# A two-layer LoRA block on one core: the transposes of a factor product moved into one group

## The chip, the cores and the metric

The kernel runs on one core of a Trainium2 chip. The metric is the device time of one execution in microseconds (us). Engines are called TensorE (PE in the rows, PEld for its weight loads), VectorE (DVE), ScalarE (ACT), GpSimd (POOL) and SyncE (SP, whose queue issues most DMA transfers).

## The reference, cut to what matters

```python
def layer0(x, ids, W, b, As, Bs):            # x: (8, 256, 1024)
    A, Bm = As[ids], Bs[ids]                 # (8, 1024, 16), (8, 16, 1024)
    return x @ W.T + b + ((x @ A) @ Bm) * 2.0

def layer1(x, ids, W, b, A_w, B_w):          # x seen as (8, 256, 1024)
    A, Bw = A_w[ids], B_w[ids]               # (8, 16, 1024), (8, 1024, 16)
    return x @ W.T + b + (x @ A.T) @ Bw.T

x = x + layer0(x, ids0, W0, b0, A0, B0)
x = x + layer1(x, ids1, W1, b1, A1, B1)
```

This is the mathematics of it; the reference writes each layer out with einsums, all in fp32.

## The kernel before, in words

The kernel folds both layers into one. With U = I + W0 and V = I + W1 (transposed), the dense part of the result is x (U V), so the product of the two weights is made once, in a weight stage, and then each of the eight batches is multiplied with it. Both products follow the Strassen-Winograd scheme with seven products of 512 x 512 quadrants. fp32 accuracy comes from splitting every operand into a high part (a cast by ScalarE to the fp32r format) and a low part (a subtraction by VectorE), and three matmuls (high x high, high x low, low x high) for each tile. Functions named `high...` are ScalarE's casts, `low...` VectorE's subtractions, `combine` VectorE's sums of quadrants.

The order of work on each engine is written out by hand, one program per engine, tied by semaphores. There is no planner. TensorE's weight stage runs M1, M2, the first G passes (L1227), M7, four transposes, M3, the small product of the factors (L1252), the r passes for the low-rank rows (L1173 to L1175), three matmuls each onto those rows (L1268 to L1270), M6, the second G passes (L1282), M5, M4. Each M is four row blocks of twelve matmuls with 512 columns. Then come the column sums of the bias (L1427), the h products of batches 0 and 1 (L1337, x times the stacked low-rank factors), and the batches, whose products are in L1305 to L1307 and L1312.

**G** is the product of U and the second layer's A factors, gathered for all eight batches. It is made transposed: the G passes leave one half at a time in bank 4 (`b_banks[0]`). ScalarE copies the half to `gt_raw` (`gt_copy`, L501, L508), TensorE turns it 128 x 128 at a time with four transposes (`turn`, L1164, L1167), and VectorE copies the result from its bank into its half of `g_all` (`g_copy`, L761, L763). `gt_raw` is one place, the second half of `g_all`, used for both halves, so the second copy of ScalarE waits for the first four transposes. `turn(0)` stands after M7 (L1239) and writes bank 0, `turn(1)` in M4 after its second row block (L1296), into bank 7. The wait ahead of `turn(1)` is for one block of d22 and one of t1 (L1294, L1295), since M5's result leaves its banks in the order 3, 1, 2, 0 (`ORDER_LAST`): ScalarE makes d22's high part (L647), VectorE its low part (L799) and t1's raw block (L800).

VectorE's `factors(b)` (L852, L860, L862) puts the first layer's A and the batch's columns of G side by side for the h product; it waits for G (`g_made`).

**The bias.** `bias_first(k)` and `bias_last(k)` add the bias of the first layer, times the rows of V, to the bias of the second: each is two VectorE instructions (L777). `bias_first(0)` and `(1)` stand before low(us4) (L979), `(2)` and `(3)` after the low part of b_sum (L1000). They read v11, whose room the sum vt2 (L1004) takes over, so that waits for all of `bias_first`.

**VectorE's order around the change.** b0_sum, bias_first(0), (1), low(us4), an e1 block (L769), low(v22), e1, b_sum, low parts of B0's factors, e1 twice, g_copy(0), low(us2), b_sum's low part, bias_first(2), (3), vt2, bias_last, then the sums of the factor product: L1011 and L1012 (t_sum), L1015. Then low(vt2), b1's low part (L1021), vt1, vt4, low_r, us1, low(u22), low(us1), the low part of A's difference (L1035), low(vt1) and so on. At the end of the stage: low(t2), low_d21(0), g_copy(1), factors(0), factors(1), low_d21(1) to (3), the low part of the column sums (L1077), low(t1).

**SP's queue.** After the weights it waits for t_sum (L350), stores it (L351), waits for its landing (L353), loads it back turned (L354), stores b1's parts ("bounce", L360, L363), loads x of batch 0 (L312), stores the r rows (L372), loads x of batch 1. ScalarE's first cast of x (L536) waits for the r bounce to have landed (L641), because it overwrites the room of the r rows.

Of the kernel before, what the change touches and what calls it, by code (L numbers as in the profile page):

```python
# [10 lines left out]
P = 128  # L11
# [3 lines left out]
DMA = 16  # L15

KH = 4
# [10 lines left out]
SLOT = {"u11": 0, "v11": 1, "u12": 2, "v21": 3, "us3": 4, "vt3": 5, "us4": 0, "v22": 2, "us2": 4, "vt2": 0,  # L28
        "us1": 1, "u22": 3, "vt1": 5, "vt4": 2, "d11": 0, "t3": 4, "t2": 5, "d21": 1, "t1": 3, "t4": 2, "d22": 6}
# [11 lines left out]
def lora_pair(nc, xT, U11, V11, W0, W1T, A0, B0T, A1T, B1, b0, b1, idx0, idx1, out):  # L41
# [5 lines left out]
    KT = 2 * KH  # L47
# [3 lines left out]
    NH = D // W0.shape[4]  # L51
# [12 lines left out]
    with ExitStack() as ctx:  # L64
# [31 lines left out]
        g_all = sb("g_all", [P, KT, BR], F32)  # L96
        a0_raw = sb("a0_raw", [P, 2, KT * RK], F32)
        s_hl = sb("s_hl", [P, 2, BR], F32R)
        ident = sb("ident", [P, P], F32)
# [32 lines left out]
        c_hl = [rows[0:NH * CT, part, :].bitcast(F32R) for part in range(2)]  # L132


        gt_raw = g_all[:, KH:KT, :].rearrange("p k n -> p (k n)")

        def raw(name):
            at = UNIT[name]
# [47 lines left out]
        def x_raw(j, b):  # L186
            return xr[b % PLACES][j // 2][:, j % 2, :] if j <= A22 else s_raw(j, b)

        banks = [ctx.enter_context(nc.psum_tensor(f"bank{i}", [P, HALF], F32)) for i in range(8)]
        a_banks, b_banks = banks[0:KH], banks[KH:2 * KH]  # L190
        LAST = (banks[0], banks[1])
        X, Z, Y, V, W = (banks[i] for i in (4, 5, 3, 2, 0))

        H_BANK = [banks[i] for i in (6, 7) + (6, 7, 1) * 2]
# [12 lines left out]
        bias1_landed = sem("bias1_landed")  # L207
# [9 lines left out]
        ident_made = sem("ident_made")  # L217
# [6 lines left out]
        summed = {q: sem(f"summed_{q}") for q in ("us1", "us2", "us3", "us4", "vt1", "vt2", "vt3", "vt4",  # L224
                                                  "t1", "t2", "t4")}
        hi = [sem(f"hi_of_place{s}") for s in range(7)]
        lo = [sem(f"lo_of_place{s}") for s in range(7)]
        m_done = {n: sem(f"m{n}_done") for n in range(1, 8)}
        m1_kept = sem("m1_kept")
        d11_kept = sem("d11_kept")  # L230
# [14 lines left out]
        gt_copied = sem("gt_copied")  # L245
        g_turned = sem("g_turned")
        g_made = sem("g_made")
# [39 lines left out]
        def filled(q, n):  # L287

            ahead = list(SLOT)[:list(SLOT).index(q)]
            return n + sum(PARTS.get(p, 1) for p in ahead if SLOT[p] == SLOT[q])  # L290
# [182 lines left out]
        def _(act):  # L473
# [27 lines left out]
            def gt_copy(h):  # L501
                act.wait_ge(gt_summed, h + 1)
                if h == 0:
                    act.wait_ge(lora_lo, 1)
                    act.wait_ge(a_diff_made, 1)
                else:
                    act.wait_ge(g_turned, 1)
                nc.scalar.copy(gt_raw, b_banks[0][:, :]).then_inc(gt_copied, 1)  # L508

            def st_copy():  # L510
                act.wait_ge(st_summed, 1)
# [137 lines left out]
            def high_d21(n):  # L649
                act.wait_ge(m_done[4], n + 1)  # L650
                nc.scalar.copy(op_k("d21", 0, ORDER_LAST[n]), a_banks[ORDER_LAST[n]][:, :]).then_inc(hi[SLOT["d21"]], 1)
# [13 lines left out]
            high("t2")  # L665
            for n in range(KH):
                high_d21(n)
            act.wait_ge(c_summed, 1)
            nc.scalar.copy(c_hl[0], Z[0:NH * CT, :]).then_inc(c_split, 1)
            act.wait_ge(summed["t1"], KH)  # L670
# [26 lines left out]
        def _(dve):  # L697
# [58 lines left out]
            def halves(v):  # L756

                v = v.rearrange("p (b k r) -> p b k r", b=B, k=KT)
                return v[:, :, 0:KH, :], v[:, :, KH:KT, :]

            def g_copy(h):  # L761
                dve.wait_ge(g_turned, h + 1)
                nc.vector.tensor_copy(g_all[:, h * KH:(h + 1) * KH, :].rearrange("p k n -> p (k n)"),  # L763
                                      (a_banks[0], b_banks[3])[h][:, :]).then_inc(g_made, 1)

            def make_e1(n):
                m = ORDER_M7[n]
# [13 lines left out]
            def bias_first(k):  # L781
                bias_add(2 * k, "v11", k, 0, b0_raw[:, k:k + 1])
                bias_add(2 * k + 1, "vt3", k, 1, b0_raw[:, k:k + 1])
# [19 lines left out]
            def low_d21(n):  # L803
                m = ORDER_LAST[n]
                dve.wait_ge(hi[SLOT["d21"]], filled("d21", n + 1))
                nc.vector.tensor_tensor(op_k("d21", 1, m), a_banks[m][:, :], op_k("d21", 0, m), ALU.subtract  # L806
                                        ).then_inc(lo[SLOT["d21"]], 1)
                nc.vector.tensor_tensor(raw_k("t4", m), a_banks[m][:, :], raw_k("t2", m), ALU.subtract  # L808
                                        ).then_inc(summed["t4"], 1)
# [120 lines left out]
            def put_c12_last():  # L930
                b = B - 1
                dve.wait_ge(kept["u4"], b + 1)
                for n in range(2):
                    cols = slice(n * HALF // 2, (n + 1) * HALF // 2)
                    dve.wait_ge(p_done[3], b + 1 + n)
                    nc.vector.tensor_tensor(c12[b % 2][:, cols], LAST[n][:, 0:HALF // 2], u4[b % 2][:, cols], ALU.add  # L936
                                            ).then_inc(made["c12"], 1)
# [11 lines left out]
            for k in range(1, KH):  # L949
# [24 lines left out]
            combine("us4", "us2", "u12", ALU.subtract)  # L974
            dve.wait_ge(b0_landed, DMA)
            nc.vector.tensor_tensor(b0_sum[:, :], b0_raw[:, 0:KH], b0_raw[:, KH:KT], ALU.add).then_inc(b0_summed, 1)
            dve.wait_ge(bias1_landed, DMA)
            dve.wait_ge(summed["vt3"], 1)
            bias_first(0)  # L979
            bias_first(1)  # L980
            dve.wait_ge(m1_kept, KH)
            low("us4")
            make_e1(0)
# [6 lines left out]
            low_factors(1)  # L990
            make_e1(2)
            make_e1(3)
            g_copy(0)
            low("us2")
            dve.wait_ge(b_sum_hi, 1)
            nc.vector.tensor_tensor(b_sums[:, :, BR:2 * BR].rearrange("p k (b r) -> p b k r", b=B),
                                    b_sum_raw.rearrange("p (b k r) -> p b k r", b=B, k=KH),
                                    b_sums[:, :, 0:BR].rearrange("p k (b r) -> p b k r", b=B), ALU.subtract
                                    ).then_inc(b_sum_lo, 1)
            bias_first(2)  # L1000
            bias_first(3)
            dve.wait_ge(lo[SLOT["v11"]], filled("v11", KH))
            dve.wait_ge(bias_step, 2 * KH)
            combine("vt2", "v11", "vt3", ALU.subtract)  # L1004
# [61 lines left out]
            low_d22(2)  # L1066
            low_d22(3)
            low("t2")
            dve.wait_ge(lo[SLOT["t3"]], filled("t3", 1))
            low_d21(0)  # L1070
            g_copy(1)
            factors(0)
            factors(1)
            for n in range(1, KH):
                low_d21(n)
            dve.wait_ge(c_split, 1)
            nc.vector.tensor_tensor(c_hl[1], Z[0:NH * CT, :], c_hl[0], ALU.subtract).then_inc(c_split, 1)  # L1077
# [55 lines left out]
        def _(pe):  # L1133
# [27 lines left out]
                    last = mm(b_banks[0][:, :], low_a, op_k(q, 0, k), start=False, stop=(stop and k == KH - 1))  # L1161
                return last

            def turn(h, bank):  # L1164
                pe.wait_ge(gt_copied, h + 1)
                for k in range(KH):
                    last = nc.tensor.transpose(bank[:, k * P:(k + 1) * P], gt_raw[:, k * P:(k + 1) * P], ident[:, :])  # L1167
                last.then_inc(g_turned, 1)

            def r_passes(rows_b, q, bank, start):  # L1170
# [16 lines left out]
            for k in range(KH):  # L1187
# [13 lines left out]
                for m in range(KH):  # L1201
# [3 lines left out]
                    last = low_passes("u11", "v11", a_banks[m], m, k)  # L1205
# [4 lines left out]
            for k in range(0, KH, 2):  # L1210
# [9 lines left out]
                for m in range(KH):  # L1220
                    for kk in (k, k + 1):
                        last = low_passes("u12", "v21", a_banks[m], m, kk, True)
# [11 lines left out]
                    pe.wait_ge(gt_copied, 1)  # L1234
                row_block("us3", "vt3", b_banks[m], m, False).then_inc(m_done[7], 1)

            pe.wait_ge(ident_made, 2)
            pe.wait_ge(d11_kept, 1)
            turn(0, a_banks[0])  # L1239


            pe.wait_ge(lo[SLOT["us4"]], filled("us4", 1))
            pe.wait_ge(lo[SLOT["v22"]], filled("v22", 1))
# [6 lines left out]
            for k in range(KT):  # L1250
                for n in range(2):
                    last = mm(a_banks[1][:, 0:2 * BR + 2], a1[:, k, n * BR:(n + 1) * BR], b0w[:, k, 0:2 * BR + 2],  # L1252
                              start=(k == 0 and n == 0), stop=(k == KT - 1 and n == 1))
            last.then_inc(st_summed, 1)

            pe.wait_ge(g_made, 1)
            r_passes(b0w[:, 0:KH, :], "v11", a_banks[0], True)
            r_passes(b0w[:, KH:KT, :], "v21", a_banks[0], False).then_inc(r_passed, 1)
            pe.wait_ge(st_copied, 1)
# [6 lines left out]
            for h in range(NH):  # L1266
                cols = slice(h * HALF, (h + 1) * HALF)
# [23 lines left out]
            for n, m in enumerate(ORDER_LAST):  # L1291
                row_block("u22", "vt4", a_banks[m], m, True).then_inc(m_done[4], 1)
                if n == 1:
                    pe.wait_ge(lo[SLOT["d22"]], filled("d22", 1))  # L1294
                    pe.wait_ge(summed["t1"], 1)  # L1295
                    turn(1, b_banks[3])  # L1296

            def product(b, x, t, bank, start):

# [121 lines left out]


            pe.wait_ge(bias_step, 2 * KT)
            pe.wait_ge(lo[SLOT["d22"]], filled("d22", KH))
            pe.wait_ge(summed["t1"], KH)
            for j in range(NH):
                last = mm(Z[j * CT:(j + 1) * CT, :], ones_b[:, 0:CT], bias_sum[:, j * CW:(j + 1) * CW],  # L1427
                          start=True, stop=True)
# [74 lines left out]
```

## Time and profile before

| | |
|---|---|
| Median of 3 runs | 281.93 us (281.27 to 282.66) |
| The profiled execution's own time | 282.09 us |
| Its span, first to last instruction | 280.5 us |
| Granted TensorE clock, mean of the span | 1.000 of full speed |
| TensorE matmul busy | 275.7 us, 98% of the span |
| VectorE busy | 214.6 us, 77% |
| ScalarE busy | 101.6 us, 36% |
| GpSimd busy | 21.7 us, 8% |
| DMA | 33.93 MB, mean 121 GB/s |

Times in the rows are microseconds from the first instruction. In a timeline row the first number is the start, the second the duration, then engine, line of the kernel and operation, output<-input, the number of instructions; what stands in brackets is the idle time of the engine before the row and what ended it. A row with x4 is four instructions, and its duration runs from the start of the first to the end of the last. Matmuls overlap: a row of 0.39 us is followed by the next after 0.23 us, so the start-to-start distance (pitch) is what a matmul costs.

### The profile page before, as it was taken

Reading aid. Unit: us, or ns where it says so; the run is one execution under the profiler, and the core shown is the slowest. Engines: PE = TensorE matmul, PEld = TensorE weight load, DVE = VectorE, ACT = ScalarE, POOL = GpSimd, SP = SyncE. Lnnn points to the kernel's source line nnn. Section 1 sums busy time; section 2 is a strip of 40 time slices with the busy share of each in tenths; the row PEclk is TensorE's granted clock in tenths of the full one; section 3 lists DMA queues with packets and bytes.
Section 4 is the critical chain, followed back from the end, with each engine's and each line's share of the span. In section 5 each row is a group of like instructions: output and inputs, shape, how many; then the busy total and the mean of one; then the engine's idle time right before and its main releaser. Section 6 shows DMA issues by size and latency. Waiting matters only on the chain.

```text
span 280.5 us, 3865 instructions
## 1 busy us (share of the span) xinstructions
PE 275.7 (98%) x1321; PEld 224.8 (80%) x1321; DVE 214.6 (77%) x321; ACT 101.6 (36%) x141; POOL 21.7 (8%) x48
## 2 busy tenths in 40 slices
PE   8999999999999999999999999999999999999995
PEld 6888887888888885888877888888877888888885
DVE  5789999999899699898982875875772865875413
ACT  4665464352964575404231223132221223132000
POOL 3333200401002001001000000000000000000000
DMA  7997000200376200293701713702802302303003
GB/s 231 395 419 294 29 1 0 60 19 0 108 268 266 110 2 9 77 348 133 241 22 65 240 56 121 232 15 114 245 1 78 132 0 112 95 2 128 22 0 150
DMA packets 13112, 33.93 MB, mean 121 GB/s; under 512 B 2165, under 2 KB 2421, under 8 KB 13094
## 3 DMA queue, kind: packets, MB, share of 16 engines
q1 hardware_dynamic: 12066, 31.60, 31.8%
q0 software_dynamic: 1024, 2.10, 2.4%
q8 instruction: 10, 0.16, 0.2%
q14 instruction: 8, 0.07, 0.1%
q10 hardware_dynamic: 4, 0.00, 0.0%
HBM read 22.09 MB, written 11.60 MB: 120 GB/s over the span
## 4 chain that ended last, share of the span: by engine, by line
PE 60%; DVE 2%; issue 0%
PE bank L1305 18%; PE bank L1306 18%; PE bank L1307 18%; PE bank L1337 3%; PE bank L1312 3%; DVE ops L739 1%; PE bank L1370 0%; PE bank L1371 0%; PE bank L1369 0%; DVE ops L806 0%; DVE g_all L763 0%; DVE raw_a L808 0%; DVE raw_a L936 0%; PE bank L1372 0%; DVE aa L862 0%
## 5 line engine op out<-in xcount | busy, mean ns | idle before, releaser
L1305 PE MATMUL bank<-ops,late 128*128 128x512 f32 x192 | 75.1, 391 | 0.0
L1306 PE MATMUL bank<-ops,late 128*128 128x512 f32 x192 | 74.8, 389 | 0.0
L1307 PE MATMUL bank<-ops,late 128*128 128x512 f32 x192 | 74.7, 389 | 0.0
L1145 PE MATMUL bank<-ops 128*128 128x512 f32 x112 | 43.6, 389 | 0.0
L1146 PE MATMUL bank<-ops 128*128 128x512 f32 x112 | 43.6, 389 | 0.0
L1305 PEld LDWEIGHTS bank<-ops,late 128*128 128x128 f32 x192 | 36.0, 188 | 8.7 <-issue 1.2
L1307 PEld LDWEIGHTS bank<-ops,late 128*128 128x128 f32 x192 | 36.0, 188 | 7.6
L1306 PEld LDWEIGHTS bank<-ops,late 128*128 128x128 f32 x192 | 36.0, 188 | 7.4
L1141 PE MATMUL bank<-ops 128*128 128x512 f32 x112 | 40.7, 398 | 0.2 <-issue 0.2
L536 ACT CAST late<-rows 128x512 fp32r<-128x512 f32 x24 | 14.7, 621 | 54.6 <-DVE rows L834 29.6
L1141 PEld LDWEIGHTS bank<-ops 128*128 128x128 f32 x112 | 21.4, 192 | 5.1 <-issue 0.4
L1145 PEld LDWEIGHTS bank<-ops 128*128 128x128 f32 x112 | 21.1, 188 | 4.4
L1146 PEld LDWEIGHTS bank<-ops 128*128 128x128 f32 x112 | 21.0, 188 | 4.4
L739 DVE TENSOR_TENSOR ops<-raw_a,ops 128x2048 fp32r<-128x2048 f32 x9 | 20.5, 2281 | 0.0
L813 DVE TENSOR_TENSOR late<-rows,late 128x512 fp32r<-128x512 f32 x24 | 16.5, 689 | 4.9 <-ACT late L536 4.8
L490 ACT CAST ops<-raw_a 128x2048 fp32r<-128x2048 f32 x9 | 17.1, 1910 | 7.7 <-DVE raw_a L742 5.2
L923 DVE TENSOR_TENSOR raw_a<-bank,raw_a 128x512 f32<-128x512 f32 x8 | 5.5, 692 | 17.6 <-PE bank L1312 17.5
L739 DVE TENSOR_TENSOR ops<-raw_b,ops 128x2048 fp32r<-128x2048 f32 x6 | 13.6, 2285 | 0.0
L490 ACT CAST ops<-raw_b 128x2048 fp32r<-128x2048 f32 x6 | 11.4, 1914 | 6.0 <-DVE raw_b L742 3.7
L813 DVE TENSOR_TENSOR late<-raw_a,late 128x512 fp32r<-128x512 f32 x15 | 10.1, 686 | 2.7 <-ACT late L536 2.6
L911 DVE TENSOR_TENSOR raw_a<-bank,raw_a 128x512 f32<-128x512 f32 x8 | 5.5, 689 | 8.5 <-PE bank L1307 8.5
L558 ACT COPY raw_a<-bank 128x512 f32<-128x512 f32 x4 | 2.4, 588 | 23.9 <-PE bank L1312 23.9
(177 smaller groups left out, 397.8 us busy)
## 6 DMA issues: line engine op xcount, KB each, us to landing
out<-raw_a SPq DMA_DIRECT2D x27, 256.0 KB, 2.3
raw_a<-xT SPq DMA_DIRECT2D x10, 512.0 KB, 6.6
a<-rb_rows SPq DMA_DIRECT2D x8, 392.0 KB
x_mid<-xT SPq DMA_DIRECT2D x6, 512.0 KB, 6.2
raw_b<-W SPq DMA_DIRECT2D x2, 1024.0 KB, 15.6
rb_rows<-b_hl SPq DMA_DIRECT2D x3, 512.0 KB
rb_rows<-late SPq DMA_DIRECT2D x3, 512.0 KB
raw_b<-V SPq DMA_DIRECT2D x4, 256.0 KB, 4.3
```

The source lines that it names most:

```text
L490: nc.scalar.copy(op(q, 0), raw(q)).then_inc(hi[SLOT[q]], 1)
L536: nc.scalar.copy(x_op(j, 0), x_raw(j, b)).then_inc(op_hi[j], 1)
L739: nc.vector.tensor_tensor(op(q, 1), raw(q), op(q, 0), ALU.subtract).then_inc(lo[SLOT[q]], 1)
L813: nc.vector.tensor_tensor(x_op(j, 1), x_raw(j, b), x_op(j, 0), ALU.subtract).then_inc(op_lo[j], 1)
L1141: return mm(bank[:, :], left(u, 0, k, m), op_k(v, 0, k), start=(k == 0 and not on_top), stop=False, skip_group_check=on_top)
L1145: mm(bank[:, :], left(u, 0, k, m), op_k(v, 1, k), start=False, stop=False, skip_group_check=on_top)
L1146: return mm(bank[:, :], left(u, 1, k, m), op_k(v, 0, k), start=False, stop=(k == KH - 1), skip_group_check=on_top)
L1305: mm(bank[:, :], hi, t_op(t, 0, k), start=(start and k == 0), stop=False, skip_group_check=not start)
L1306: mm(bank[:, :], hi, t_op(t, 1, k), start=False, stop=False, skip_group_check=not start)
L1307: last = mm(bank[:, :], lo, t_op(t, 0, k), start=False, stop=(k == KH - 1), skip_group_check=not start)
L1312: return mm(bank[:, :], h_stack[b % 2][:, q * P:(q + 1) * P], rb[b % 2][:, h * HALF:(h + 1) * HALF], start=False, stop=True, skip_group_ch ...
L1337: last = mm(bank[j * CT:(j + 1) * CT, 0:T], of_b[:, k, :], xr[at][kh][:, :, tok], start=(k < TILES), stop=(k >= KT - TILES))
```

## The change

Both halves of G get a place of their own in `g_all`, each the place where its turned form will lie. ScalarE's second copy out of bank 4 no longer waits for a transpose. The four transposes after M7 go away, and with them M3's and the r passes' dealings with bank 0; all eight stand in M4 after its second row block, and write banks 5 and 7. The wait ahead of them is for two blocks of d22 and t1 in place of one. Both copies of the turned halves move from VectorE to ScalarE, after its second d21 cast. The column sums, which write bank 5, wait for them. On VectorE `bias_first(0)` and `(1)` move behind b_sum's low part, to the other two; `factors(0)` and `(1)` move ahead of `low_d21(0)`.

```diff
-        gt_raw = g_all[:, KH:KT, :].rearrange("p k n -> p (k n)")
+        gt_raw = [g_all[:, h * KH:(h + 1) * KH, :].rearrange("p k n -> p (k n)") for h in range(NH)]
...
+        TURNED = (banks[5], banks[7])
...
@@ ScalarE, gt_copy(h)
                 if h == 0:
                     act.wait_ge(lora_lo, 1)
                     act.wait_ge(a_diff_made, 1)
-                else:
-                    act.wait_ge(g_turned, 1)
-                nc.scalar.copy(gt_raw, b_banks[0][:, :]).then_inc(gt_copied, 1)
+                nc.scalar.copy(gt_raw[h], b_banks[0][:, :]).then_inc(gt_copied, 1)
...
@@ ScalarE, end of the weight stage
             for n in range(KH):
                 high_d21(n)
+                if n == 1:
+                    act.wait_ge(g_turned, 1)
+                    for h in range(NH):
+                        nc.scalar.copy(gt_raw[h], TURNED[h][:, :]).then_inc(g_made, 1)
...
@@ VectorE
-            def g_copy(h):
-                dve.wait_ge(g_turned, h + 1)
-                nc.vector.tensor_copy(g_all[:, h * KH:(h + 1) * KH, :].rearrange("p k n -> p (k n)"),
-                                      (a_banks[0], b_banks[3])[h][:, :]).then_inc(g_made, 1)
...
-            dve.wait_ge(bias1_landed, DMA)
-            dve.wait_ge(summed["vt3"], 1)
-            bias_first(0)
-            bias_first(1)
             dve.wait_ge(m1_kept, KH)
             low("us4")
...
             make_e1(3)
-            g_copy(0)
             low("us2")
...
-            bias_first(2)
-            bias_first(3)
+            dve.wait_ge(bias1_landed, DMA)
+            dve.wait_ge(summed["vt3"], 1)
+            for k in range(KH):
+                bias_first(k)
...
             low("t2")
-            dve.wait_ge(lo[SLOT["t3"]], filled("t3", 1))
-            low_d21(0)
-            g_copy(1)
             factors(0)
             factors(1)
-            for n in range(1, KH):
+            dve.wait_ge(lo[SLOT["t3"]], filled("t3", 1))
+            for n in range(KH):
                 low_d21(n)
...
@@ TensorE
-            def turn(h, bank):
-                pe.wait_ge(gt_copied, h + 1)
-                for k in range(KH):
-                    last = nc.tensor.transpose(bank[:, k * P:(k + 1) * P], gt_raw[:, k * P:(k + 1) * P], ident[:, :])
+            def turn():
+                pe.wait_ge(gt_copied, NH)
+                for h in range(NH):
+                    for k in range(KH):
+                        cols = slice(k * P, (k + 1) * P)
+                        last = nc.tensor.transpose(TURNED[h][:, cols], gt_raw[h][:, cols], ident[:, :])
                 last.then_inc(g_turned, 1)
...
-            pe.wait_ge(ident_made, 2)
-            pe.wait_ge(d11_kept, 1)
-            turn(0, a_banks[0])
...
-            pe.wait_ge(g_made, 1)
             r_passes(b0w[:, 0:KH, :], "v11", a_banks[0], True)
...
                 if n == 1:
-                    pe.wait_ge(lo[SLOT["d22"]], filled("d22", 1))
-                    pe.wait_ge(summed["t1"], 1)
-                    turn(1, b_banks[3])
+                    pe.wait_ge(lo[SLOT["d22"]], filled("d22", 2))
+                    pe.wait_ge(summed["t1"], 2)
+                    pe.wait_ge(ident_made, 2)
+                    turn()
...
             pe.wait_ge(bias_step, 2 * KT)
+            pe.wait_ge(g_made, NH)
             pe.wait_ge(lo[SLOT["d22"]], filled("d22", KH))
```

## Rows read from the trace of the kernel before

**Rows 1.** The page, part 1: busy time, share of the span, instructions.

```profile
PE 275.7 (98%) x1321; PEld 224.8 (80%) x1321; DVE 214.6 (77%) x321; ACT 101.6 (36%) x141; POOL 21.7 (8%) x48
```

**Rows 2.** TensorE's waits: line, releaser, us in total, times, longest.

```profile
PE bank L1337 <- DVE aa L862: 0.5, 1, 0.5
```

**Rows 3.** Timeline of TensorE, 43 to 45 us: transposes, then M3.

```profile
43.67 0.60 PE L1167 MATMUL bank<-ident,g_all 128*128 128x128 f32 x4
44.48 0.47 PE L1141 MATMUL bank<-ops 128*128 128x512 f32 x1 [0.21 <-issue]
```

**Rows 4.** Timeline of VectorE, 36 to 44 us: bias steps, low(us4), low(v22).

```profile
36.65 2.73 DVE L777 SCALAR_TENSOR_TENSOR rows<-raw_b,b_raw,rows 128x512 f32<-128x512 f32 x4
39.30 2.28 DVE L739 TENSOR_TENSOR ops<-raw_a,ops 128x2048 fp32r<-128x2048 f32 x1
...
42.10 2.28 DVE L739 TENSOR_TENSOR ops<-raw_a,ops 128x2048 fp32r<-128x2048 f32 x1
```

**Rows 5.** Timeline of ScalarE, 36 to 39 us: the cast of us4.

```profile
36.69 1.92 ACT L490 CAST ops<-raw_a 128x2048 fp32r<-128x2048 f32 x1 [3.11 <-DVE raw_a L742]
```

**Rows 6.** Timeline of VectorE, 47 to 56 us: G's copy, low(us2), vt2.

```profile
47.92 0.68 DVE L763 COPY g_all<-bank 128x512 f32<-128x512 f32 x1
48.51 2.28 DVE L739 TENSOR_TENSOR ops<-raw_a,ops 128x2048 fp32r<-128x2048 f32 x1
...
54.15 2.29 DVE L742 TENSOR_TENSOR raw_b<-raw_b 128x2048 f32<-128x2048 f32 x1
```

**Rows 7.** Timeline of VectorE, 64 to 80 us: low parts of b1, of A's difference.

```profile
64.59 1.22 DVE L1021 TENSOR_TENSOR b_hl<-rows,b_hl 128x1024 fp32r<-128x1024 f32 x1
...
78.82 0.68 DVE L1035 TENSOR_TENSOR a<-factor_sums,a 128x512 fp32r<-128x512 f32 x1
```

**Rows 8.** Timeline of TensorE, 68 to 81 us: low-rank rows, second G passes.

```profile
68.28 0.39 PE L1268 MATMUL bank<-b_hl,s_hl 128*128 128x512 f32 x1
...
80.52 0.39 PE L1159 MATMUL bank<-ops,a 128*128 128x512 f32 x1
```

**Rows 9.** Timeline of SP's queue, 62 to 82 us: t_sum, its way back, r bounce.

```profile
62.04 0.36 SPq L351 DMA_DIRECT2D t_sums<-t_sum  x1
69.78 0.33 SPq L354 DMA_DIRECT2D t_cols<-t_sums  x1
...
78.00 3.83 SPq L360 DMA_DIRECT2D rb_rows<-late  x3
```

**Rows 10.** Timeline of ScalarE, 94 to 104 us: first x casts, d21 casts.

```profile
94.16 1.67 ACT L536 CAST late<-raw_a 128x512 fp32r<-128x512 f32 x3 [4.91 <-DMA rb_rows<-late]
...
103.22 1.08 ACT L651 CAST ops<-bank 128x512 fp32r<-128x512 f32 x2
```

**Rows 11.** Timeline of VectorE, 101 to 117 us: t1's second block, d21, low(t1).

```profile
101.01 0.68 DVE L800 TENSOR_TENSOR raw_a<-bank,raw_a 128x512 f32<-128x512 f32 x1
...
107.41 0.68 DVE L806 TENSOR_TENSOR ops<-bank,ops 128x512 fp32r<-128x512 f32 x1
...
114.11 2.27 DVE L739 TENSOR_TENSOR ops<-raw_a,ops 128x2048 fp32r<-128x2048 f32 x1
```

**Rows 12.** Timeline of TensorE, 102 to 110 us: transposes, column sums, h product.

```profile
102.28 0.60 PE L1167 MATMUL bank<-ident,g_all 128*128 128x128 f32 x4
102.64 0.48 PE L1141 MATMUL bank<-ops 128*128 128x512 f32 x1
...
103.88 0.39 PE L1146 MATMUL bank<-ops 128*128 128x512 f32 x1
...
108.28 1.05 PE L1427 MATMUL bank<-rows,ones_b 128*32 128x512 f32 x4
109.79 1.07 PE L1337 MATMUL bank<-raw_a,aa 128*32 128x256 f32 x16 [0.45 <-DVE aa L862]
```

**Rows 13.** Timeline of TensorE, 2 to 5 us: matmuls on zeros before the work.

```profile
2.22 2.87 PE L1184 MATMUL bank<-c_rows 128*128 128x512 f32 x6
```

**Rows 14.** The cores: span and mean granted TensorE clock.

```profile
core 0: 280.5 us, clock 1.000
```

## The prediction

> **What bounds the kernel now.** The page first: TensorE is busy for 98% of the span [rows 1], so nothing matters that doesn't move TensorE's row of matmuls. Next the list of TensorE's waits: after the start only one of size is in it, 0.5 us in the h products, for VectorE's factors [rows 2]. From about 112 us on TensorE runs without a wait up to the last store, so what the change is worth is the time at which the first h product starts, 109.79 today [rows 12]. Third the timelines of all queues from 36 to 112 us, to see how much room lies under TensorE, and there is little. M3 starts at 44.48, 0.10 after VectorE's low part of v22 ends (42.10 + 2.28 = 44.38) [rows 3, 4]: a wait for VectorE, hidden in the hole of the transposes. From 68.28 to 80.52 lie 54 matmuls, so the pitch (start to start) is 0.227 [rows 8]. Below, "+" is later than in this trace.
>
> **Part 1, the first four transposes leave their place before M3.** The group starts at 43.67, M3 at 44.48 [rows 3]: a hole of 0.81 us. Without it M3 could begin at 43.67, if its operands are there. On VectorE four bias steps take 36.65 to 39.30; then come low(us4), one e1 block and low(v22) at 42.10 [rows 4]. With the bias steps gone, low(us4) waits for ScalarE's cast of us4, which ends at 36.69 + 1.92 = 38.61 [rows 5]. It starts at 38.65, only 0.65 earlier, though 2.65 us of work left its front: the other 2.0 us lay in ScalarE's shadow and were free. low(v22) then ends at 43.73 and M3 starts about 43.83: **-0.65** for TensorE.
>
> **Part 2, VectorE's other half.** Gone before low(us2) is the copy of G's first half, 48.51 - 47.92 = 0.59 [rows 6]. Added before vt2's sum, which waits for them, are the four bias steps, 2.65 as above. So vt2 starts at 54.15 - 0.65 - 0.59 + 2.65 = 55.56: **VectorE is +1.40** from there. Up to 94 us it has no pause that could absorb this; the only ones are waits for a ScalarE that itself waits for VectorE's sums, and for bounces of SP's queue (below), and these move along.
>
> **Part 3, who waits for a VectorE that is 1.40 late.** (a) The matmuls of the low-rank rows need b1's low part, 64.59 + 1.22 + 1.40 = 67.21; TensorE comes at 68.28 - 0.65 = 67.63 [rows 7, 8]. 0.4 us of room. (b) The second G passes follow M6 and need the low part of A's difference, which ends at 78.82 + 0.68 + 1.40 = 80.90 [rows 7]. TensorE comes at 80.52 - 0.65 = 79.87 [rows 8], waits 1.1 us and starts about 81.00: **+0.48**. What part 1 gained is gone here, however much it was. (c) SP stores the row t_sum at 62.04, right behind VectorE's step that makes it. The landing lets it go on at 69.78 with the b1 bounce and x, and the r bounce is issued from 78.00 [rows 9]. ScalarE's first x cast waits for that bounce until 94.16, 4.91 idle [rows 10]. Each issue stands behind the one before, so SP's queue moves by 1.40, and with it ScalarE and VectorE from 94 to 110 us, where VectorE has no idle time. Whether landings keep their length when all is moved, nothing in the trace says; the ends are no shift and 1.40. I take 1.40, since SP sits at t_sum's landing from 62.4 to 69.8.
>
> **Part 4, the group of eight in the middle of M4.** Today four transposes start at 102.28, the next matmul at 102.64, and the sixth of the matmuls at 103.88 [rows 12], where an unbroken row would have had it at 102.28 + 5 x 0.227 = 103.41. Four cost 0.47, of which 0.36 is their own pitch of 0.09. Eight cost 0.83, **+0.36**. The new wait is for t1's second block: VectorE ends it at 101.01 + 0.68 = 101.69 today [rows 11], at 103.09 then. With the lag of 0.10 the group starts at 103.19, **+0.91**; without that wait it would start +0.48. The column sums, 108.28 today [rows 12], start at 108.28 + 0.91 + 0.36 = 109.55. The Trainium skill (TensorE: Matmul & The Clock Gate, Part 4: PE-mode transpose) has about 275 ns for one transpose in a kernel. The pitch in this trace disagrees with taking that as a cost per transpose; eight at 0.275 would be 1.4 us more, and the sum 283.8.
>
> **Part 5, the end of the stage.** ScalarE's first two d21 casts end at 103.22 + 1.08 + 1.40 = 105.70 [rows 10]; two copies of G at its 0.54 pitch end at 106.8, and its third d21 cast has to wait for TensorE's third block until about then. So they cost nothing; without that cover each would delay the next cast by 0.5. VectorE's order becomes low(t2), factors, d21 blocks. low(t2) is over at 107.41 + 1.40 = 108.81 [rows 11] and G is there since 106.8, so the factors of batch 0 are ready at 109.2, before TensorE wants them. The wait of 0.45 ahead of 109.79 is thus gone. How long the column sums hold up the h product that wait has covered: between four pitches of 0.15 (0.6) and their whole row, 1.05 [rows 12]. So the h product starts between 110.15 and 110.60, +0.36 to +0.81. I take +0.45, near the pitch, because everywhere in this trace TensorE goes on by pitch. Behind it VectorE is +1.40 less the copy of G's second half, 0.60: t1's low part ends at 114.11 + 2.27 + 0.8 = 117.2 [rows 11], and the product that reads it starts 36 matmuls after 112.1, at 120.3. Enough room; nothing else in the batches changes.
>
> **Sum.** +0.45 on a profiled execution of 282.09 is 282.54. It lies 0.16 above the median of the three runs, so against the median it is **282.4 us**.
>
> **Rival A, SP's queue isn't late** (the landing is set by something that doesn't move). For it: t_sum, 128 words, takes 69.78 - 62.04 = 7.7 us [rows 9], as if held up by something else. Against it: the other transfers of these microseconds are few, and nothing is named that could hold it. The Trainium skill (DMA: Bandwidth & Descriptors, Anatomy of one DMA) gives a fixed cost of about 2 us for a transfer, which this row exceeds. Then t1's second block is ready at 101.69, TensorE keeps the +0.48 of (b), the column sums start at 109.12, the h product at 109.7 to 110.2: 281.9 to 282.3.
>
> **Rival B, the full gain.** VectorE's 1.40 is absorbed before 78 us, and neither (b) nor (c) waits: -0.65 + 0.36 = -0.29 at the column sums, the h product at 108.6 to 109.0, 280.7 to 281.2. Against it: [rows 6, 7] show VectorE without a pause of its own to absorb it in.
>
> **Rival C, slower.** Place: the landing of the r bounce, issued from 78.00 to 81.83 and landed at 94.1, 12 us after its last issue [rows 9, 10]. It decides from a delay of nothing on, because the chain bounce, cast, d22, t1's second block now ends on TensorE's new wait, with nothing between. If it lands 1 us later than the shift, all is 1 us later, 283.4; with 2 us, 284.4. For it: the runs of before differ by 1.4 us, as such landings could make them. Against it: the transfers of that queue move together, so no new collision is in sight.
>
> **Rival D, the clock.** TensorE gets two new pauses, 1.1 us in (b) and 0.4 us before the group. If the granted clock fell to its level of 1.2 GHz after one, matmuls would go at the pitch of the six at the start, (2.87 - 0.65) / 5 = 0.445 [rows 13], 0.22 more each; ten would cost 2.2 us, 284.6. Against it: the pause of 0.45 [rows 12] is followed by full pitch, and the granted clock is 1.000 over the span [rows 14].
>
> **How the numbers follow.** A measurement of this kernel can tell about 0.5% from no change, 1.41 us: faster is below 280.5, slower above 283.3. Chances: forecast 0.57 (its own range 282.1 to 283.1), A 0.15, B 0.08, C 0.17, D 0.03. B itself lies within 0.5% but near its edge; the half of it that goes with some further gain, and as much for a gain unseen, make 0.07 for faster. C from 0.9 us on, D and a cost unseen make 0.16 for slower. The rest, 0.77, is within. The range goes from 281.0, the middle of B, to 283.9, the middle of C.
>
> **What would show it.** No transposes before M3, and M3 at about 43.8; vt2's sum at 55.5; TensorE pausing 1.1 us behind the low part of A's difference, on at 81.0; t_sum stored at 63.4 and ScalarE's first x cast at 95.6; eight transposes at 103.2, behind t1's second block; the h product at 110.2 with no wait for factors; batches of unchanged length. The forecast is wrong if the second G passes start before 80.6, if the first x cast isn't late, or if the h product waits for its factors.

## The result

The changed kernel takes 282.87 us (median of 22 runs, 282.08 to 286.13), the kernel before 282.07 in the same session (22 runs, 281.21 to 282.92). The ratio is 1.0049 with a 95% interval of 1.0036 to 1.0062: slower by 0.8 us in the medians, 1.2 in the means and 1.4 going by the ratio. There is a tail that the kernel before doesn't have: five of the 22 executions are above 283.8. The forecast was 282.4 us, "within 0.5%" at 0.77. It holds, but at the edge of what it called no change.

The profiled execution is one of the tail: 285.43 us, span 283.9. Busy times and waits of TensorE (line, releaser, us in total, times, longest), to be held against [rows 1, 2]:

```profile
PE 276.3 (97%) x1321; PEld 224.1 (79%) x1321; DVE 213.3 (75%) x319; ACT 102.4 (36%) x143; POOL 21.7 (8%) x48
...
PE bank L1164 <- DVE late L799: 2.0, 1, 2.0
...
PE bank L1154 <- DVE a L1032: 1.0, 1, 1.0
```

The wait for the factors is gone; two new ones stand in its place. L1164 is the group of eight transposes, L1154 the second G passes. Now the changed kernel's timelines, in the order of the forecast's steps. VectorE (against [rows 4, 6, 7]):

```profile
39.37 2.29 DVE L744 TENSOR_TENSOR ops<-raw_a,ops 128x2048 fp32r<-128x2048 f32 x1 [1.97 <-ACT ops L492]
...
50.80 5.38 DVE L777 SCALAR_TENSOR_TENSOR rows<-raw_b,b_raw,rows 128x512 f32<-128x512 f32 x8
56.28 2.29 DVE L747 TENSOR_TENSOR raw_b<-raw_b 128x2048 f32<-128x2048 f32 x1
...
80.96 0.68 DVE L1032 TENSOR_TENSOR a<-factor_sums,a 128x512 fp32r<-128x512 f32 x1
```

The 1.97 us of idle time ahead of low(us4) are the shadow in which the two bias pairs used to lie for nothing. TensorE (against [rows 3, 8, 12]):

```profile
44.57 0.47 PE L1136 MATMUL bank<-ops 128*128 128x512 f32 x1 [0.33 <-issue]
...
81.79 0.47 PE L1154 MATMUL bank<-ops,a 128*128 128x512 f32 x1 [1.00 <-DVE a L1032]
...
105.83 1.06 PE L1164 MATMUL bank<-ident,g_all 128*128 128x128 f32 x8 [2.03 <-DVE late L799]
106.65 0.48 PE L1136 MATMUL bank<-ops 128*128 128x512 f32 x1
...
112.30 0.62 PE L1422 MATMUL bank<-rows,ones_b 128*32 128x512 f32 x2
112.33 0.63 PE L1331 MATMUL bank<-raw_a,aa 128*32 128x256 f32 x4
112.75 0.60 PE L1422 MATMUL bank<-rows,ones_b 128*32 128x512 f32 x2
...
115.01 0.50 PE L1299 MATMUL bank<-ops,late 128*128 128x512 f32 x1
```

SP's queue and ScalarE's first x cast (against [rows 9, 10]):

```profile
64.18 0.36 SPq L353 DMA_DIRECT2D t_sums<-t_sum  x1
71.57 0.33 SPq L356 DMA_DIRECT2D t_cols<-t_sums  x1
...
79.70 3.49 SPq L362 DMA_DIRECT2D rb_rows<-late  x3
...
98.20 1.66 ACT L536 CAST late<-raw_a 128x512 fp32r<-128x512 f32 x3 [7.58 <-DMA rb_rows<-late]
```

**Two yardsticks.** One execution starts some tenths later than another, because the weights land when they land: VectorE's first sum of quadrants (us3, which waits for one of them) starts at 18.15 in the first trace of before, at 18.81 in this one, at 17.99 to 19.36 over all traces. So I count from that sum. And from the first x product (L1299 here, 115.01) to the end it's 285.43 - 115.01 = 170.42 us, 170.4 to 170.5 in every one of the fourteen traces: the batches aren't touched by any of this. What is left to compare is the stretch from that sum to the first x product: 93.50 before (111.65 - 18.15), 96.20 here.

On that scale M3 is at 44.57 - 18.81 = 25.76 where before had 26.33 (-0.57; forecast -0.65), vt2 is +1.47 (forecast +1.40), the second G passes +0.61 (forecast +0.48), t_sum's store +1.48. The pause ahead of the group is 2.03 us. The r bounce was issued by 83.19 and ScalarE's cast starts at 98.20, 15.0 us later, where before had 12.3.

### The profile page after: what moved, and what is told of

Read it like the earlier page. It is cut to its first block, busy times and chain, and to the rows that moved or that the text cites. A ratio compares the mean times of both kernels' runs of the same rounds, so it can differ in the third digit from the quotient of the medians.

```text
span 283.9 us, 3865 instructions
## 1 busy us (share of the span) xinstructions
PE 276.3 (97%) x1321; PEld 224.1 (79%) x1321; DVE 213.3 (75%) x319; ACT 102.4 (36%) x143; POOL 21.7 (8%) x48
## 4 chain that ended last, share of the span: by engine, by line
PE 62%; DVE 1%; issue 0%
PE bank L1299 18%; PE bank L1300 18%; PE bank L1301 18%; PE bank L1331 3%; PE bank L1306 2%; PE bank L1141 1%; PE bank L1136 1%; PE bank L1140 1%; DVE late L813 0%; PE bank L1164 0%; PE bank L1365 0%; PE bank L1364 0%; PE bank L1363 0%; PE bank L1422 0%; DVE rows L850 0%
## 5 line engine op out<-in xcount | busy, mean ns | idle before, releaser
L1299 PE MATMUL bank<-ops,late 128*128 128x512 f32 x192 | 75.1, 391 | 0.0
L1299 PEld LDWEIGHTS bank<-ops,late 128*128 128x128 f32 x192 | 36.0, 188 | 8.7 <-issue 1.2
L744 DVE TENSOR_TENSOR ops<-raw_b,ops 128x2048 fp32r<-128x2048 f32 x6 | 13.6, 2283 | 0.0
L536 ACT CAST late<-raw_a 128x512 fp32r<-128x512 f32 x15 | 9.1, 621 | 7.6 <-DMA rb_rows<-late 7.6
```

Of the source, the lines that this page charges most:

```text
L536: nc.scalar.copy(x_op(j, 0), x_raw(j, b)).then_inc(op_hi[j], 1)
L744: nc.vector.tensor_tensor(op(q, 1), raw(q), op(q, 0), ALU.subtract).then_inc(lo[SLOT[q]], 1)
L1299: mm(bank[:, :], hi, t_op(t, 0, k), start=(start and k == 0), stop=False, skip_group_check=not start)
```

## The experiments

Each was built on the changed kernel, or on the kernel before where that is said. Medians are of all executions beside the kernel before in the same session (281.9 to 282.2).

**The bias steps back.**

```diff
+            dve.wait_ge(bias1_landed, DMA)
+            dve.wait_ge(summed["vt3"], 1)
+            bias_first(0)
+            bias_first(1)
             dve.wait_ge(m1_kept, KH)
             low("us4")
...
-            for k in range(KH):
-                bias_first(k)
+            bias_first(2)
+            bias_first(3)
```

> The changed kernel with bias_first(0) and (1) back ahead of low(us4). Theory (the 2.65 us of bias work, 2.0 of them moved out of ScalarE's shadow, make VectorE late, and TensorE waits for it twice): M3 starts at about 44.5 again, VectorE is 0.6 us earlier than in the kernel before (no copy of G), the second G passes start without a wait, the group of eight starts without a wait or nearly so, and the column sums are +0.36 against before; h product -0.5 to -0.1: 281.6 to 282.0 us, at least 0.8 below the changed kernel. Rival 1 (the group of eight itself is what costs): about 282.9, as the changed kernel. Rival 2 (the late SP queue has nothing to do with VectorE's t_sum): first x cast as late as in the changed kernel.

Measured 282.02 us (11 runs) against 281.96, ratio 1.0002 (0.9988 to 1.0016). There's no wait at the G passes and none at the group; the trace has 93.25 us from the sum to the first x product, 0.25 less than before. So with the bias steps in their old place the rest of the change costs nothing, and the loss is theirs. The first x cast comes 12.3 us after the last issue of the bounce.

**The kernel before, with the bias steps moved alone** (both pairs from ahead of low(us4) to behind b_sum's low part).

> The kernel before with the two bias steps moved behind b_sum's low part and nothing else. Theory: VectorE is +2.0 us from vt2 on (2.65 less the 0.65 by which low(us4) starts earlier; here the copy of G stays), the first x cast and the end of VectorE's chain are +2.0, TensorE waits for the low part of A's difference (+1.1) and then for the factors: h product +2.0, 284.1 us. M3 starts behind the first transposes at about 44.1. Rival 1 (the group of eight costs, the bias steps don't): 282.1. Rival 2 (SP's queue doesn't follow VectorE): h product at about 110.3 to 110.7 by the G passes alone, 282.6 to 283.0.

Measured 283.53 us (6 runs), ratio 1.0059 (1.0045 to 1.0073). From the trace: 95.05 us from sum to first x product, +1.55. VectorE's part of A's difference comes 2.1 us later on this scale, TensorE waits for it and again for the factors:

```profile
PE bank L1157 <- DVE a L1033: 1.2, 1, 1.2
...
PE bank L1335 <- DVE aa L862: 0.7, 1, 0.7
```

The forecast of +2.0 was high by the landings: t_sum is stored 2.09 later on this scale, as forecast, but lands in 7.3 us, 0.4 quicker than in the first trace of before, and the bounce 0.1 quicker. Both rivals fall: the bias steps do cost, and SP's queue does follow VectorE.

**SP's order.** The wait for t_sum's landing and the load behind it go behind the r bounce.

```diff
-            sp.wait_ge(zeroed, 2)
-            sp.wait_ge(t_bounced, DMA)
-            sp.dma_start(t_cols[RK:2 * RK, :], t_dram.rearrange("(b r) o -> r (b o)", r=RK), ...)
...
             bounce(0, r_hl, r_bounced)
+            sp.wait_ge(zeroed, 2)
+            sp.wait_ge(t_bounced, DMA)
+            sp.dma_start(t_cols[RK:2 * RK, :], t_dram.rearrange("(b r) o -> r (b o)", r=RK), ...)
             load_x(1)
```

> The changed kernel with SP's wait for t_sum's landing, and the load behind it, moved behind the r bounce. Theory: the b1 bounce goes out when b1 is split, at about 68, 3.5 us earlier; the r bounce lands 3 us or more earlier, the first x cast is at about 92 to 93, and t1's second block is ready before TensorE gets there. The group of eight doesn't wait, TensorE keeps +0.48 from the second G passes and +0.36 from the four more transposes: h product 109.7 to 110.2, 281.9 to 282.3 us, and no executions at 285. Rival (landing times are set by something else, the queue's order doesn't matter): first x cast not earlier, 282.9 us and single executions at 285 as in the changed kernel.

The first x cast comes at 91.62, 73.0 after the sum against 76.0 before: 3 us earlier, as expected. The group starts without a pause at 103.44. But the median is 282.77 (7 runs, up to 284.04), ratio 1.0038 (1.0023 to 1.0053), not 282.1. Sum to first x product is 93.97. So the pause ahead of the group can't be what an ordinary execution of the changed kernel loses. And one of the seven is above 283.8 though this order hides the bounce, so its late landings needn't be the whole tail.

**The group after the third row block** (`if n == 2` in place of `if n == 1`).

> The changed kernel with the group of eight after the third row block of M4 in place of the second. Theory: the wait for t1's second block is hidden by 2.7 us of matmuls; column sums +0.84 in place of +1.27 in an execution with an undelayed bounce; h product 109.7 to 110.2: 282.0 to 282.4 us, and in an execution with a late bounce up to 2.4 us less. Rival (the wait only moves to the factors or to the column sums' wait for G): 282.9 us, the same as the changed kernel, with a wait ahead of the h product.

Measured 282.88 us (6 runs), ratio 1.0039 (1.0025 to 1.0053): no better than the changed kernel. In its trace there was no wait to be hidden:

```profile
102.12 0.68 DVE L800 TENSOR_TENSOR raw_a<-bank,raw_a 128x512 f32<-128x512 f32 x1
...
106.12 1.03 PE L1164 MATMUL bank<-ident,g_all 128*128 128x128 f32 x8
106.91 0.48 PE L1136 MATMUL bank<-ops 128*128 128x512 f32 x1
```

t1's second block (L800) ends at 102.80, and TensorE passes the group's old place at 106.12 - 12 x 0.227 = 103.40, 0.6 us later. The trace has 94.00 us from sum to first x product, with one new pause only, 1.0 us at the G passes. It serves as the trace of an ordinary execution, for want of one of the changed kernel itself: all three traces of that have a late bounce. The rival's price was right, but not by its mechanism: there's no wait ahead of the h product either.

**The changed kernel again.**

> The changed kernel once more, for the trace of an ordinary execution: the traced one took 285.4 us where the median is 282.9, with the r bounce landing 15 us after its last issue. Theory (that execution is slow by the landing alone, which now ends on TensorE's wait for t1's second block): median 282.9; from TensorE's first x product to the end 170.4 us as in every trace so far; in an execution near the median, the first x cast at 95 to 96, the pause behind A's difference about 1.0, and no pause or under 0.5 ahead of the group of eight. Rival (the wait ahead of the group is there in every execution): a pause of 1 us or more there in an execution of 282.9.

Median 282.95 us (12 runs, 282.34 to 286.98), ratio 1.0034 (1.0015 to 1.0053). The traced execution took 284.25: the bounce took 13.6 us from the last issue (97.01), and the pause ahead of the group is 0.97. So the pause grows with the landing: 0 at 12.3, 0.97 at 13.6, 2.03 at 15.0. Whether an execution near the median pauses there, this trace can't say.

**The group twice**, sixteen transposes (`turn` gets a flag, and only its second call signals that G is turned).

```diff
-                    turn()
+                    turn(False)
+                    turn(True)
```

> The changed kernel with the group of eight transposes done twice, one after the other. Theory: a transpose costs its pitch of 0.09 us, eight more cost 0.72: 283.6 us, and the group's own row goes from 0.8 to 1.5 us. Rival (they cost their duration, about 0.27 each, where they stand in one group): 2.2 more, 285.1. Rival 2 (they lie beside a wait): 282.9.

Measured 283.78 us (8 runs), 0.8 to 0.9 above the changed kernel. One execution took 287.96, with a mean granted clock of 0.994. VectorE's step for t1's second block, the matmul ahead of the group, the group and the matmul behind it in the same trace:

```profile
103.14 0.68 DVE L800 TENSOR_TENSOR raw_a<-bank,raw_a 128x512 f32<-128x512 f32 x1
...
103.33 0.39 PE L1141 MATMUL bank<-ops 128*128 128x512 f32 x1
103.92 1.94 PE L1164 MATMUL bank<-ident,g_all 128*128 128x128 f32 x16 [0.20 <-issue]
105.62 0.48 PE L1136 MATMUL bank<-ops 128*128 128x512 f32 x1
```

Sixteen take 1.70 start to start, eight take 0.79 in the trace of the kernel with the group after the third row block: 0.10 to 0.11 each, not the 0.27 of their duration. The 275 ns of the Trainium skill (TensorE: Matmul & The Clock Gate, Part 4: PE-mode transpose) is the length of such a row here as well (0.27); it isn't what one costs in a group. The mean granted clock of that execution is 1.000, sixteen transposes in a row included.

This trace also has the wait that the forecast put ahead of the group, though its bounce landed on time (12.5 us). The profile names no releaser for it ("issue"), but t1's second block ends at 103.14 + 0.68 = 103.82, and the group starts 0.10 later, where the pitch would have had it at 103.33 + 0.227 = 103.56: 0.36 us start to start, forecast 0.43. Here t_sum had taken 8.06 us to land, against 7.25 in the trace before. The stretch adds up with it: 94.00 + 0.91 for eight more transposes + 0.36 = 95.27, and it measures 95.28.

**One bias pair back**, the other three together.

```diff
+            dve.wait_ge(bias1_landed, DMA)
+            dve.wait_ge(summed["vt3"], 1)
+            bias_first(0)
             dve.wait_ge(m1_kept, KH)
             low("us4")
...
-            for k in range(KH):
-                bias_first(k)
+            bias_first(1)
+            bias_first(2)
+            bias_first(3)
```

> The changed kernel with bias_first(0) back ahead of low(us4), where VectorE waits 2.0 us for ScalarE and two steps of 0.66 fit, and bias_first(1) to (3) left where the change has them. Theory: VectorE is at +0.1 from vt2 on against before, M3 still starts 0.65 earlier, the second G passes don't wait, the group costs +0.36, the wait for the factors is gone, and the column sums lie open at about 0.85 (two traces have shown that): first x product at 110.7 in place of 111.65, 281.1 us. Rival (the four more transposes and the open column sums eat it): 281.9, as the kernel before.

Measured 281.42 us (12 runs, 281.15 to 282.43) against 281.92, ratio 0.9980 (0.9967 to 0.9993): **faster than both kernels**, by 0.5 and by 1.5 us (a small gain, but its interval leaves out 1, and the next kernel repeats it). VectorE and TensorE in its trace:

```profile
36.56 1.41 DVE L777 SCALAR_TENSOR_TENSOR rows<-raw_b,b_raw,rows 128x512 f32<-128x512 f32 x2
38.62 2.29 DVE L744 TENSOR_TENSOR ops<-raw_a,ops 128x2048 fp32r<-128x2048 f32 x1 [0.65 <-ACT ops L492]
```

```profile
43.70 0.40 PE L1143 MATMUL bank<-ops 128*128 128x512 f32 x1
43.93 0.39 PE L1138 MATMUL bank<-ops 128*128 128x512 f32 x1
...
101.64 1.03 PE L1166 MATMUL bank<-ident,g_all 128*128 128x128 f32 x8
...
110.78 0.50 PE L1301 MATMUL bank<-ops,late 128*128 128x512 f32 x1
```

The pair fits into ScalarE's shadow, 0.65 us of which is still free, and low(us4) starts as early as without it. After the start TensorE has no wait at all in this trace: M3 (L1138) follows M7 at the ordinary pitch, and 92.72 us lie between sum and first x product, 0.78 less than before.

**The same, with SP's new order.**

> As the split kernel, and SP's wait for t_sum's landing moved behind the r bounce. Theory: the median as the split kernel, 281.1 (TensorE doesn't wait for the bounce in either at the median), but no execution above 282, since the first x cast comes 2.5 us earlier and a late landing is covered. Rival (the spread of the executions comes from elsewhere): the same spread as the split kernel.

Measured 281.42 us (12 runs, 281.13 to 282.35), ratio 0.9977 (0.9965 to 0.9989): as the split kernel, and with the same spread. Where VectorE isn't late, the order of SP's queue buys nothing; the split kernel had no tail to take away.

**The kernel before again.**

> The kernel before once more, for a second trace of it: in the first one VectorE's first sum of quadrants (us3) started at 18.15, in the traces of the changed kernel at 18.5 to 18.8. Theory (the weights land some tenths earlier or later in each execution, whatever the kernel): 281.9 to 282.1 us; the distance from that sum to the first x product is again 93.5 us, give or take 0.5 for the landing of the r bounce, with the wait for the factors. Rival (the changed kernel starts later for a reason of its own): the sum at 18.2 or less again.

Median 281.79 us (12 runs). The traced execution (283.48) has the sum at 19.35 and the first x product 93.67 later, with 0.61 us of wait for the factors. So the stretch is the same as in the first trace, and the start isn't the kernel's doing.

**The split kernel with the column sums twice** (`for j in tuple(range(NH)) * 2:`).

> The split kernel with the column sums of the bias made twice, into the same place. Theory (open, they cost their length on TensorE, 0.85): 0.85 more than the split kernel's 281.4, 282.3 us. Rival (they cost four pitches of 0.15, as I took it for the forecast): 0.6 more, 282.0.

Measured 282.55 us (12 runs) against 282.22 for the kernel before in that session. The split kernel was 0.50 below its own reference, this one is 0.33 above: 0.83 more. The two intervals are about 0.4 us wide to either side, so the medians alone don't tell 0.85 from 0.6; the traces do: 3.57 us from the start of the sums to the first x product (112.05 - 108.48) against 2.71 (110.78 - 108.07), 0.86 more. The first rows of the sums and of the h product:

```profile
108.48 1.48 PE L1424 MATMUL bank<-rows,ones_b 128*32 128x512 f32 x6
109.38 0.41 PE L1333 MATMUL bank<-raw_a,aa 128*32 128x256 f32 x2
```

**The changed kernel, a third trace.**

> The changed kernel, one more look, for a trace of an ordinary execution. Theory: if the r bounce lands 12 to 12.5 us after its last issue, there is no pause ahead of the group of eight beyond 0.2, and the pause behind A's difference stands alone; from VectorE's first us3 sum to the first x product 93.9 to 94.1 us. Rival: a pause ahead of the group of 0.4 or more also then, as forecast.

This one execution took 287.84 us, and isn't ordinary: the bounce took 15.1 us (cast at 99.03), and TensorE paused 2.93 ahead of the group. What came then is the forecast's rival D. The rows are those of TensorE, then the windows (busy time by engine, granted clock, DMA share, GB/s):

```profile
106.66 1.06 PE L1164 MATMUL bank<-ident,g_all 128*128 128x128 f32 x8 [2.93 <-DVE late L799]
107.48 0.56 PE L1136 MATMUL bank<-ops 128*128 128x512 f32 x1
107.85 0.63 PE L1140 MATMUL bank<-ops 128*128 128x512 f32 x1
108.27 0.63 PE L1141 MATMUL bank<-ops 128*128 128x512 f32 x1
```

```profile
106.00:108.00 2.00, 1.34 (x10) 1.28 (x11) 2.00 (x4) 2.00 (x2) 0.00 (x0) 0.93 0.00 0
108.00:110.00 2.00, 2.00 (x7) 1.51 (x6) 2.00 (x4) 2.00 (x5) 0.00 (x0) 0.50 0.03 8
110.00:112.00 2.00, 2.00 (x8) 1.63 (x7) 2.00 (x2) 0.14 (x1) 0.00 (x0) 0.71 0.00 0
```

After the pause the granted clock goes to 0.50, 1.2 GHz, and the pitch of the matmuls from 0.227 to 0.43. From 107.48 the nine matmuls of this stretch take 3.73 us (to 111.21); in the first trace of the changed kernel the same nine take 2.16 (106.65 to 108.81). That's 1.6 us on top of the pause. The mean granted clock of this execution is 0.994; the longest two of the other 34 executions of the changed kernel, 286.13 and 286.98, have the same 0.994, and no other has less than 0.998.

**The kernel before with one pair moved.**

> The kernel before with one step pair, bias_first(1), moved behind b_sum's low part, and the transposes and copies of G as before. Theory (the split kernel wins only because the copies of G are off VectorE and the wait for the factors is gone): VectorE is 0.65 earlier at low(us4) and 1.33 later behind it, +0.68; M3 starts 0.4 earlier, but the end of VectorE's chain, factors and h product are +0.68 behind the same start: 282.6 us. Rival (placing one pair in ScalarE's shadow is the whole gain of the split kernel): 281.4.

Measured 282.83 us (12 runs) against 281.98, ratio 1.0023 (1.0008 to 1.0038). TensorE waits 0.27 at the G passes and 0.69 for the factors; sum to first x product is 112.33 - 18.58 = 93.75. On the stretch that's only 0.1 to 0.25 more than the two traces of before: t_sum is stored 0.75 later on this scale, but lands in 7.46 us, against 7.74 and 8.04. The same split that wins in the changed kernel loses here, so it's not the bias pair by itself. What else it takes is argued and not isolated: the copies of G leave VectorE, which takes 0.59 out of its row in front of the G passes and another 0.6 out of it in front of the factors; but the merged transposes and the new place of the factors come with them.

## Why the prediction was right, and where it wasn't

The sign and the range held. The size held on the trace of an ordinary execution (the group after the third row block, 94.00), +0.50 on the stretch where the forecast was +0.45; in the medians it's +0.80, nearly twice that. By its own steps:

- **Part 1** was right: M3 0.57 earlier instead of 0.65. The gain is lost at the second G passes, as said.
- **Part 2** was right: VectorE +1.47 instead of +1.40, with low(us4) held by ScalarE for 1.97 us. This is the cause of the loss, shown from both sides: putting the steps back takes the loss away (1.0002), moving them alone in the kernel before makes 1.0059.
- **Part 3 (b)** was right: +0.61 on the common scale instead of +0.48, and +0.65 in the ordinary trace. It left out the restart: the second matmul behind the pause comes after 0.31 us (81.55 to 81.86 there) and not 0.227, 0.08 more.
- **Part 3 (c)** was right that SP's queue is late by as much as VectorE. t_sum takes 7.2 to 8.1 us to land in all twelve traces in which SP waits for it, stored earlier or later, so rival A falls. The 2 us that the forecast holds against this row from the Trainium skill (DMA: Bandwidth & Descriptors, Anatomy of one DMA) are given there for transfers of GpSimd's path; t_sum goes out on SP's queue, so the row doesn't contradict that figure. Why it takes so long stays open.
- **Part 4** put a wait of 0.43 us ahead of the group in every execution. That step failed. In the ordinary trace there is none: counted from the start sum, t1's second block ends at 84.27 where the forecast had 84.94 (t_sum landed in 7.25 us instead of 7.74, and the store of it isn't all of the chain), and TensorE comes at 84.87 instead of 84.61. In the trace with sixteen transposes it is there, 0.36, with t_sum landed in 8.06. So a wait of 0.43 was read off two chains that end within tenths of each other, and whose landings vary by more than that. The median doesn't hold it: hiding it, by SP's order or by the third row block, leaves 282.77 and 282.88. The price of the group was nearly right, 0.43 more instead of 0.36.
- **Part 5** undersized the column sums. Open, they cost 0.85 (2.71 us from their start to the first x product, against 1.86 from the start of the h product before), not the 0.69 that the +0.45 implied (110.24 - 109.55). That lies midway between the bounds of 0.6 and 1.05. The pitch of the four rows is no guide, since the h product's first matmuls start between them but don't get ahead by it.

So the sum came out by luck, because errors met. Against the ordinary trace there's 0.43 us too much in the wait ahead of the group, and 0.17 too little at the G passes, 0.08 for the restart behind them, 0.07 in the group's price and 0.16 at the sums. That leaves 0.05.

The medians differ by 0.8 to 1.0, the traces by 0.5. A little of this is the tail. In its traces it is **rival C** with **rival D** behind it: at 1.3 to 2.8 us of extra landing TensorE pauses 1.0 to 2.9 us ahead of the group, and after the longest pause the clock takes 1.6 more. (Rival D's price per matmul was near, 0.43 for 0.445, but the six matmuls that it was read from run at a granted clock of 1.00 in their windows; only this execution shows what the lower clock costs.) The chance of the two was put at 0.17 and 0.03 for the median; it was really a matter of one execution in four or five (9 of 35 above 283.8, three of them the profiled ones). Without those nine the medians are 282.74 and 282.76, so the tail makes 0.1 to 0.2 of the difference. The rest, 0.2 to 0.3 us beyond the trace's 0.5, stays open: kernels on the changed order had it too (bias steps back: 0.25 less than before by the trace, but equal by the median). Two traces of the kernel before may not be enough to say what its ordinary stretch is, and a profiled execution isn't always a typical one: in three of the experiments it is the slowest of its set, in one the fastest.

What also stays open is why the bounce lands late at all. With SP's order as it is, it took 12.2 to 12.5 us in nine traces and 13.6 to 15.1 in three, all three of the changed kernel as it stands and none of its variants; with SP's new order 13.4 and 14.0, hidden. The issue times don't tell them apart (79.70, 79.93 and 80.20 where it was late, 79.25 and 80.29 where it was on time). Nor does the load on the DMA engines: from 90 to 94 us they are busy for half the time (0.50 to 0.52) in the three late traces as in three on time.

## What to carry to other kernels

Before moving work off the front of an instruction, ask whether that instruction can start earlier at all: 2.0 of the 2.65 us taken out here had been free behind another engine's cast, and became 1.4 us on the path. Fill such a shadow to its length and move only what sticks out: that turned a loss of 0.8 us into a gain of 0.5. And a step that gives up its slack to a transfer has the transfer's spread as its own, in the worst executions with a slower clock behind the pause.

## What wasn't expected of the hardware

In one trace a pause of 2.93 us between full-rate matmuls was followed by a granted clock of 0.50 for 3.7 us of work; pauses of 2.03 and 1.0 in other executions weren't (granted clock 1.00 in their windows). 128 words stored to DRAM by one transfer took 7.2 to 8.1 us to land in the twelve traces in which SP waits for it, more than three times the 2.3 us of a 256 KB store. And two fp32 matmuls of 32 x 512 (four rows in the trace) cost 0.85 us of TensorE, nearly as much as four of the split kind with 128 x 512 (4 x 0.227).
